# One scan step for both batches, with single large matmuls among its small tile products, in an RWKV-6 attention kernel

## The chip, the cores and the metric

The program runs on one core of one Trainium2 chip. The metric is the device time of one execution in microseconds (us). A core has five engines that run side by side and wait for each other through semaphores: PE (TensorE, matrix products into the PSUM banks), DVE (VectorE), ACT (ScalarE), POOL (GpSimd) and SP, which here only starts transfers.

## The reference

Two batches of 4096 tokens with 512 channels pass an attention layer and a feed-forward layer. Only the attention is touched. Cut to what matters:

```python
xw, xk, xv, xr, xg = [x + sx * mix[:, :, i] for i in range(5)]   # sx: the token before minus this one
r, k, v = xr @ Wr, xk @ Wk, xv @ Wv
g = jax.nn.silu(xg @ Wg)
w = jnp.exp(-jnp.exp(time_decay + jnp.tanh(xw @ td_w1) @ td_w2))
def step(state, rkvw):                     # 4096 tokens, 16 heads of 32 channels
    a = k_t[..., :, None] * v_t[..., None, :]
    y = jnp.einsum('bhk,bhkv->bhv', r_t, state + u[None, :, :, None] * a)
    new_state = w_t[..., :, None] * state + a
    return (new_state, y)
return normalised(y) * g @ Wo              # then x + ga * this, and the feed-forward layer
```

## The kernel before

The attention handles 32 chunks of 128 tokens, each for both batches. Iteration i of every engine's loop works on three chunks: it projects chunk i, runs the scan of chunk c = i - 1, and finishes chunk f = i - 2 (output product, residual). Each engine runs a fixed program; the order of its work is the order in which the body functions call the helpers, and semaphores hold it together.

The scan is done by groups of 32 tokens. Step n = 0 to 7 takes batch n // 4 and group n % 4. `pe_scores` multiplies keys by queries in 32x32 tiles of the array: 16 products of 80 columns (L406), 16 each of 48 and 16 (L410, L412), and 16 for the state's increment (L417), 64 in all. `dve_A` then assembles the 32x32 matrices `Am` from these scores with one product (L874) and seven predicated copies (L887), and updates the state (L881, L903). `pe_y` forms the output of the group in 32 tile products (L432, L435). The scores of odd and even n go to different PSUM banks (`SC[n % 2]`, `XB[n % 2]`), and `pe_scores(n)` waits for the assembly of n - 1 alone, so that scores for one step are formed while DVE assembles the one before.

Among the steps stand, on PE, whole 128x128 products: the g projection (`pe_g`, L512, two halves of eight matmuls), the output product (`pe_wo`, L525, four matmuls of 512 columns for each batch), the mixing products `pe_delta` (L466) and two decay products (L479, L486). After the steps come the transposes `pe_x` (L444), the k, r and v projections (L498), `pe_tm1` (L451, L454) and the scores of step 0 for the next iteration:

```python
            for n in range(1, 8):
                if do_w:
                    pe_scores(pe, c, n)
                    if n <= 2:
                        pe_g(pe, c, n - 1, do_p)
                    pe_y(pe, c, n - 1)
```

DVE's order around step 0 matters too: at the end of an iteration it transposes keys (L861), scales and transposes the normalised output (L920, L922), and only then begins the steps. The product with the gate, `dve_z` (L927), waits for ACT's affine step (L611).

Of the kernel before, what the change touches and what calls it, by code (L numbers as in the profile page):

```python
# [137 lines left out]
def attention(nc, x1, x, maa_x, maa, tm_w1, tm_w2, decay, td_w1, td_w2, faaaa, Wr, Wk, Wv, Wg, Wo,  # L138
              ln_w, ln_b, c_in, wmod, ident_in, diag_in, pick_in, ni=NI):
    with ExitStack() as ctx:  # L140
# [56 lines left out]
        s_tmp = sb("s_tmp", [P, G, K])  # L197
        Am = sb("Am", [P, 2, G, 32])
# [158 lines left out]
        score_done = sig("score_done", 8)  # L357
        A_step = sig("A_step", 8 * A_STEPS)
        A_done = sig("A_done", 8)
        s_step = sig("s_step", 8)  # L360
        state_done = sig("state_done", 8)
        y_done = sig("y_done", 8)
# [33 lines left out]
        def pe_scores(pe, c, n):  # L396
            b, q = divmod(n, Q)
            sc, scm = SC[n % 2], XB[n % 2]
            if n == 0:
                settled_after(pe, mod_done, (der, c), (ru_done, c), (m1_done, c), (k_done, c), (derk, c, 2))  # L400
            elif n >= 2:
                settled_after(pe, mod_done, (A_done, c, n - 1))
            for g in range(G):
                X = (g * B + b) * Q + q
                for d in HEADS:
                    nc.tensor.matmul(sc[d, g * NS:(g + 1) * NS], kvar[d, 0, g, b, 32 * q:32 * q + 32], rcol[d, X, 0:M1], start=True, stop=True)  # L406
            for g in range(G):
                X = (g * B + b) * Q + q
                for d in HEADS:
                    nc.tensor.matmul(scm[d, g * NM:g * NM + X0 - M1], kvar[d, 1, g, b, 32 * q:32 * q + 32], rcol[d, X, M1:X0], start=True, stop=True)  # L410
                for d in HEADS:
                    nc.tensor.matmul(scm[d, g * NM + X0 - M1:(g + 1) * NM], kvar[d, 2, g, b, 32 * q:32 * q + 32], rcol[d, X, X0:SEND], start=True, stop=True)  # L412
            if n == 0:
                settled_after(pe, mod_done, (vT_done, c), (kT_done, c))
            for g in range(G):
                for d in HEADS:
                    last = nc.tensor.matmul(sc[d, G * NS + g * K:G * NS + (g + 1) * K], kT[d, g, b, q, :], v_s[d, g, b, q, :], start=True, stop=True)  # L417
            last.then_inc(score_done.sem, 1)

        def pe_y(pe, c, n):  # L420
            b, q = divmod(n, Q)
            if n == 0:
                settled_after(pe, mod_done, (A_done, c, n + 1), (yT_done, c - 1))
            elif n == 4:
                settled_after(pe, mod_done, (A_done, c, n + 1), (yT_done, c, 1))
            else:
                settled_after(pe, mod_done, (A_done, c, n + 1))
            for g in range(G):
                X = (g * B + b) * Q + q
                for d in HEADS:  # L430
                    out = YB[d, g * P + 32 * q:g * P + 32 * q + 32]
                    nc.tensor.matmul(out, v_s[d, g, b, q, :], Am[d, n % 2, g, :], start=True, stop=False)  # L432
                for d in HEADS:
                    out = YB[d, g * P + 32 * q:g * P + 32 * q + 32]
                    last = nc.tensor.matmul(out, state[d, b, q, g, :], r32[d, X, :], start=False, stop=True)  # L435
            last.then_inc(y_done.sem, 1)
# [65 lines left out]
        def pe_g(pe, c, h, do_p):  # L502
            if h == 0:
# [12 lines left out]
        def pe_wo(pe, f, b, fenced, gated):  # L516
# [5 lines left out]
            if b == 1:  # L522
                after(pe, x1_done, f, 1)
# [1190 lines left out]
```

## Time and profile before

| | |
|---|---|
| median of 3 runs | 4346.82 us (4338.47 to 4366.6) |
| profiled execution | 4355.78 us, its span 4353.8 us |
| granted PE clock over the span | 0.931 of full speed |
| busy: PE, PE weight loads, DVE | 3775.7, 2595.8, 3517.6 us |
| busy: ACT, POOL | 1612.9, 1140.0 us |
| instruction queue | 538 packets, 8.81 MB |

The attention ends shortly after 2600 us; what follows is the preparation and the loop of the feed-forward layer. Every fp32 matmul shows as two records (two passes), each with its weight load, so 16 matmuls are "x32". Idle time with "issue" as its releaser is time in which the profile shows nothing that the engine waited for.

### The profile page before, as it was taken

To read this page: it belongs to the slowest core of one execution; us is meant where nothing else is said; L and a number is where in the kernel's file an instruction comes from. 1 tells how busy PE (TensorE), PEld (TensorE's weight loads), DVE (VectorE), ACT (ScalarE), POOL (GpSimd) and SP (SyncE) were. 2 spreads that over 40 slices of the span, in tenths; PEclk is the share of its full clock that TensorE was granted. 3 is DMA by queue.
4 is the path that set the end of the run, shared out by engine and by line. 5 is a ranking of instruction groups with operands and counts; after the bars stand their busy time and mean duration, and the time that the engine had idled before them with its cause. 6 is when DMAs were issued, how large, how long until landed. Compare 5 with 4: busy or idle time off the path is not lost. (4 is left out here: it accounts for less than half of the span.)

```text
span 4353.8 us, 155632 instructions
## 1 busy us (share of the span) xinstructions
PE 3775.7 (87%) x65992; PEld 2595.8 (60%) x65992; DVE 3517.6 (81%) x7798; ACT 1612.9 (37%) x3173; POOL 1140.0 (26%) x736
## 2 busy tenths in 40 slices
PE   4888898888898888888888873299999999999999
PEld 3767777676677776777767651145454545545454
DVE  4777788776788876788777757799999999999997
ACT  2434434344353442443434412233333333333333
POOL 1121121211212212122121113433333333333332
PEclk7989999999999998999999986599999999999999
DMA  3000000000000000000000003001011110111110
GB/s 112 13 22 27 18 32 18 23 27 18 23 27 23 27 18 23 27 21 29 18 23 27 13 22 114 15 23 37 31 37 32 36 38 30 37 30 37 38 30 30
DMA packets 73617, 133.45 MB, mean 31 GB/s; under 512 B 13248, under 2 KB 14016, under 8 KB 72896
## 3 DMA queue, kind: packets, MB, share of 16 engines
q1 hardware_dynamic: 72896, 123.13, 8.8%
q8 instruction: 538, 8.81, 0.9%
q14 instruction: 183, 1.50, 0.1%
HBM read 89.56 MB, written 33.55 MB: 28 GB/s over the span
## 5 line engine op out<-in xcount | busy, mean ns | idle before, releaser
L719 POOL TENSOR_TENSOR xf<-xf,hT 128x1024 f32<-128x1024 f32 x128 | 308.8, 2413 | 1190.6 <-DVE xf L769 1190.6
L887 DVE COPY_PREDICATED Am<-pick,banks 128x64 f32<-128x64 uint8 (+2 forms) x1792 | 459.6, 257 | 128.2 <-DVE Am L887 12.7
L1603 PE MATMUL fbank<-dT,hqT 128*128 128x512 f16 x2112 | 489.0, 380 | 20.8 <-ACT hqT L1520 20.6
L1591 PE MATMUL fbank<-gT,xqT 128*128 128x464 f16 (+1 forms) x2304 | 491.0, 363 | 11.5 <-issue 6.7
L1591 PE MATMUL fbank<-uT,xqT 128*128 128x464 f16 (+1 forms) x2304 | 488.2, 362 | 0.0
L730 POOL TENSOR_TENSOR yrs<-yvar,neg_half 128x32 f32<-128x32 f32 x32 | 174.0, 5438 | 839.7 <-DVE yvar L916 839.7
L1591 PEld LDWEIGHTS fbank<-gT,xqT 128*128 128x128 f16 x2304 | 225.6, 98 | 248.5 <-issue 12.6
L1531 ACT ACTIVATE sil<-fbank,und 128x464 f32<-128x464 f32 (+1 forms) x192 | 123.9, 646 | 656.6 <-PE fbank L1591 656.6
L1591 PEld LDWEIGHTS fbank<-uT,xqT 128*128 128x128 f16 x2304 | 225.7, 98 | 231.5 <-issue 1.1
L1603 PEld LDWEIGHTS fbank<-dT,hqT 128*128 128x128 f16 x2112 | 196.5, 98 | 236.2 <-ACT hqT L1520 31.4
L769 DVE SCALAR_TENSOR_TENSOR xf<-banks,col_maa,sx 128x256 f32<-128x256 f32 x640 | 265.3, 476 | 80.9 <-PE banks L466 80.8
L525 PE MATMUL banks<-w_o,yn 128*128 128x512 f32 x512 | 279.8, 696 | 18.0 <-DVE yn L927 15.9
L512 PE MATMUL banks<-xf,w_g 128*128 128x256 f32 x1024 | 266.9, 419 | 13.3 <-ACT gu L668 11.9
L1388 POOL TENSOR_TENSOR hq<-q16h,s16h 128x1408 f16<-128x1408 f16 x64 | 163.7, 2558 | 400.3 <-DVE hq L1380 400.3
L498 PE MATMUL banks<-xf,w_k 128*128 128x256 f32 x1024 | 251.0, 401 | 6.8 <-issue 5.0
L432 PE MATMUL banks<-Am,v_s 32*32 32x32 f32 x8192 | 191.9, 198 | 69.4 <-issue 67.8
L592 ACT ACTIVATE m_stack<-xxx 32x256 fp32r<-32x256 f32 x512 | 211.9, 414 | 99.5 <-DVE xxx L760 81.1
L435 PE MATMUL banks<-r,state 32*32 32x32 f32 x8192 | 191.9, 196 | 58.9 <-issue 58.8
L623 ACT ACTIVATE xxx<-xxx 128x1024 f32<-128x1024 f32 x32 | 33.8, 1057 | 563.0 <-DVE xxx L782 563.0
L512 PEld LDWEIGHTS banks<-xf,w_g 128*128 128x128 f32 x1024 | 208.9, 209 | 49.9 <-ACT gu L668 13.4
L874 DVE TENSOR_TENSOR Am<-banks,diag 128x128 f32<-128x128 f32 x256 | 72.3, 282 | 205.1 <-PE banks L417 200.8
L406 PE MATMUL banks<-rcol,kvar 32*32 32x80 f32 x8192 | 209.5, 238 | 25.1 <-issue 25.1
(237 smaller groups left out, 8483.3 us busy)
## 6 DMA issues: line engine op xcount, KB each, us to landing
x_tok<-in_L_attn_x SPq DMA_DIRECT2D x32, 512.0 KB, 3.8
xres<-in_L_attn_x SPq DMA_DIRECT2D x32, 512.0 KB, 3.5
x_after_attention<-xres SPq DMA_DIRECT2D x32, 512.0 KB, 3.7
xl<-x_after_attention SPq DMA_DIRECT2D x64, 256.0 KB, 2.7
xr<-x_after_attention SPq DMA_DIRECT2D x64, 256.0 KB, 2.7
out<-xr SPq DMA_DIRECT2D x64, 256.0 KB, 2.0
raw_g<-in_L_ffn_w_gate SPq DMA_DIRECT2D x1, 2816.0 KB, 10.9
raw_u<-in_L_ffn_w_up SPq DMA_DIRECT2D x1, 2816.0 KB, 14.0
```

What stands on the lines that cost most here:

```text
L406: nc.tensor.matmul(sc[d, g * NS:(g + 1) * NS], kvar[d, 0, g, b, 32 * q:32 * q + 32], rcol[d, X, 0:M1], start=True, stop=True)
L432: nc.tensor.matmul(out, v_s[d, g, b, q, :], Am[d, n % 2, g, :], start=True, stop=False)
L435: last = nc.tensor.matmul(out, state[d, b, q, g, :], r32[d, X, :], start=False, stop=True)
L498: last = nc.tensor.matmul(PROJ[h][:, (g % 2) * BT:(g % 2 + 1) * BT], w[:, k, g * P:(g + 1) * P], buf[:, k].rearrange("p b t -> p (b t)"), ...
L512: last = nc.tensor.matmul(SMALL[:, (g % 2) * BT:(g % 2 + 1) * BT], w_g[:, k, g * P:(g + 1) * P], xf[:, NMIX - 1, k].rearrange("p b t -> p ...
L525: last = nc.tensor.matmul(SMALL[:], yn[:, k, b, :], w_o[:, b, k, :], start=(k == 0), stop=(k == G - 1))
L592: last = nc.scalar.activation(m_stack[rows, j, :], m_part[part % 2][HEADS[f], 0, :], ACT.Copy)
L719: nc.gpsimd.tensor_tensor(xf[:, j % NXF].rearrange("p g b t -> p (g b) t"), xf[:, j % NXF].rearrange("p g b t -> p (g b) t"), hT[:, :, :, ...
L769: last = nc.vector.scalar_tensor_tensor(xf[:, j % NXF, g], PROJ[g // 2][:, (g % 2) * BT:(g % 2 + 1) * BT].rearrange("p (b t) -> p b t", b= ...
L887: nc.vector.copy_predicated(dst, mask, src).then_inc((done or A_step).sem, 1)
L1591: last = nc.tensor.matmul(GU[2 * pair + t][:, 0:w], xqT[:, u, a, g, :], W[:, b_, g, lo_:hi_], start=(k == 0), stop=(k == 3 * G - 1))
L1603: last = nc.tensor.matmul(DN[1 - u][:], hqT[:, a, kk, :], dT[:, b_, kk, :], start=(first and kk == 0), stop=(end and kk == KF - 1))
```

## The change

A scan step now takes one group of 32 tokens for both batches, so there are four steps q = 0 to 3 and not eight. `SC[0]`, `SC[1]` hold the scores of batch 0 and 1, `XB` is one bank for both, and `YB` becomes two banks, one per batch. `pe_scores(q)` waits for the assembly of q - 1. DVE's operations of a step are as many as before and twice as wide. `pe_g` and `pe_wo` give one matmul per call, and `pe_scores` and `pe_y` call them through `large(x)`, at eight places of a step. The copies of the output from PSUM (`act_yT`) both come after the last step, and the first half of the k projection moves behind the last step and the transposes.

```diff
-        PROJ, SC, YB = bank[2:4], bank[4:6], bank[7]
-        XB = (bank[0], bank[6])
-        XT = (bank[1], bank[6])
+        PROJ, SC, YB = bank[2:4], bank[4:6], bank[6:8]
+        XB = bank[0]
+        XT = (bank[1], bank[0])
...
+        def pe_scores(pe, c, q, large=None):
...
+            else:
+                settled_after(pe, mod_done, (A_done, c, q))
+            t = slice(32 * q, 32 * q + 32)
+            for b in range(B):
+                for g in range(G):
+                    X = (g * B + b) * Q + q
+                    for d in HEADS:
+                        nc.tensor.matmul(SC[b][d, g * P:g * P + NS], kvar[d, 0, g, b, t], rcol[d, X, 0:M1], start=True, stop=True)
...
+                    if large and g == 1:
+                        large(2 * b)
+                if large and b == 0:
+                    large(1)
...
+                if large and b == 0:
+                    large(3)
             last.then_inc(score_done.sem, 1)
...
+                    if g % 2:
+                        if b == 1 and g == G - 1:
+                            last.then_inc(y_done.sem, 1)
+                        if large:
+                            large(4 + 2 * b + g // 2)
...
+        def pe_g(pe, c, h, x, do_p):
+            if x == 0:
+                if h == 0:
+                    xf_wait(pe, c, NMIX - 1)
+                    after(pe, x1_done, c - 2)
+                    if do_p:
+                        after(pe, mf_done, c + 1)
+                else:
+                    after(pe, gu_done, c, 1)
+            g, k = 2 * h + x // 4, x % 4
+            last = nc.tensor.matmul(SMALL[:, (g % 2) * BT:(g % 2 + 1) * BT], w_g[:, k, g * P:(g + 1) * P],
...
+            def third(x):
+                if do_p and x == 1:
+                    pe_delta(pe, i, 3)
+                if do_f and x % 2:
+                    pe_wo(pe, f, 0, x // 2, do_p, do_w)
+
+            def fourth(x):
+                if do_f:
+                    pe_wo(pe, f, 1, x - 4, do_p, do_w)
+
             if do_p:
-                pe_proj(pe, i, 1, lambda h: after(pe, ww_done, i), (0,))
+                pe_delta(pe, i, 0)
             if do_w:
-                pe_y(pe, c, 7)
+                pe_scores(pe, c, 1, lambda x: pe_g(pe, c, 0, x, do_p))
+                pe_y(pe, c, 0, lambda x: pe_g(pe, c, 0, x, do_p))
+            if do_p:
+                pe_delta(pe, i, 1)
+            if do_w:
+                pe_scores(pe, c, 2, lambda x: pe_g(pe, c, 1, x, do_p))
+                pe_y(pe, c, 1, lambda x: pe_g(pe, c, 1, x, do_p))
+            if do_p:
+                pe_delta(pe, i, 2)
+                pe_td1(pe, i)
+            if do_w:
+                pe_scores(pe, c, 3, third)
+                pe_y(pe, c, 2, third)
...
+            if do_p:
+                pe_delta(pe, i, 4)
+            if do_w:
+                pe_y(pe, c, 3, fourth)
...
+            if do_p:
+                pe_td2(pe, i)
             if more:
                 pe_x(pe, i + 1)
             if do_p:
-                pe_proj(pe, i, 1, lambda h: after(pe, ww_done, i), (1,))
+                pe_proj(pe, i, 1, lambda h: after(pe, ww_done, i))
...
-            for n in range(8):
+            for q in range(Q):
                 if do_w:
-                    dve_A(dve, c, n)
-                if n == 1 and do_f:
+                    dve_A(dve, c, q)
+                if q == 0 and do_f:
                     dve_z(dve, f)
-                if 1 <= n <= 5 and do_p:
-                    dve_mix(dve, i, n - 1)
-                if n == 2 and more:
+                if do_p and q < 3:
+                    dve_mix(dve, i, q)
+                if q == 1 and more:
                     dve_ln(dve, i + 1)
-                if n == 4 and do_w:
+                if q == 2 and do_w:
                     dve_g(dve, c)
-                if n == 5 and do_f:
+                if q == 3 and do_f:
                     dve_out(dve, f, 0)
-                if n == 6 and do_p:
+                if do_p and q >= 2:
+                    dve_mix(dve, i, q + 1)
+                if q == 3 and do_f:
+                    dve_out(dve, f, 1)
+                if q == 3 and do_p:
                     dve_ww(dve, i)
```

PE's program from the scores of step 0 to the g projection, before (`banks<-v_s,kT` is L417's product, `[waits ...]` names semaphores):

```order
L417 MATMUL banks<-v_s,kT 32x32 [waits kT_done,vT_done,mod_done]
L417 MATMUL banks<-v_s,kT 32x32 x15
L406 MATMUL banks<-rcol,kvar 32x80 x16
...
L417 MATMUL banks<-v_s,kT 32x32 x16
L97 REGISTER_ALU
L512 MATMUL banks<-xf,w_g 128x256 [waits mf_done,x1_done,xf_done_p]
L512 MATMUL banks<-xf,w_g 128x256 x7
L116 ISA
L432 MATMUL banks<-Am,v_s 32x32 [waits yT_done,A_done,mod_done]
```

The same place of the changed program:

```order
L422 MATMUL banks<-v_s,kT 32x32 [waits kT_done,vT_done,mod_done]
L422 MATMUL banks<-v_s,kT 32x32 x31
L97 ISA [waits vT_done]
L473 MATMUL banks<-m_stack,w_tm 128x256 [waits m_stacked]
L473 MATMUL banks<-m_stack,w_tm 128x256 x3
L406 MATMUL banks<-rcol,kvar 32x80 [waits A_done,mod_done]
...
L410 MATMUL banks<-rcol,kvar 32x48 x4
L412 MATMUL banks<-rcol,kvar 32x16 x4
L97 REGISTER_ALU
L519 MATMUL banks<-xf,w_g 128x256 [waits mf_done,x1_done,xf_done_p]
L410 MATMUL banks<-rcol,kvar 32x48 x4
```

Before, step 1's scores and eight g matmuls stood between step 0's scores and the first wait for `A_done`. Now only one mixing product does, and the g matmuls stand one by one behind that wait. In a chunk PE goes from small tiles to a large product 25 times, before 9 times.

DVE's program of a step, before and then changed:

```order
L874 TENSOR_TENSOR Am<-banks,diag 128x128 [waits y_done,score_done]
L881 TENSOR_TENSOR s_tmp<-state,T 128x128 [waits state_done]
L108 ISA
L887 COPY_PREDICATED Am<-pick,banks 128x8x12 [waits A_step,mod_used]
```

```order
L900 TENSOR_TENSOR Am<-banks,diag 128x256 [waits y_done,score_done]
L906 TENSOR_TENSOR s_tmp<-state,T 128x256 [waits state_done]
L108 ISA
L912 COPY_PREDICATED Am<-pick,banks 128x16x12 [waits A_step,mod_used]
```

The operations of a step are the same, at twice the width, and there are four steps in a chunk.

## Rows read from the trace of the kernel before

**Rows 1.** The page's busy tenths and PE clock in 40 slices of the span.
```profile
PE   4888898888898888888888873299999999999999
PEclk7989999999999998999999986599999999999999
```

**Rows 2.** The line L910, once per chunk: duration min/median/max, first and last start.
```profile
L910 DVE STREAM_TRANSPOSE yS<-yT x32: 1235/1239/1246, 177.1 to 2602.2; 128x1024 f32<-128x1024 f32 x32
```

**Rows 3.** Busy time by stretch: length, PE, PEld, DVE, ACT, POOL, clock, DMA, GB/s.
```profile
177.10:2602.20 2425.10, 2112.08 (x55060) 1704.61 (x55057) 1852.63 (x4748) 965.24 (x2270) 485.09 (x209) 0.93 0.07 22
```

**Rows 4.** PE's waits in that stretch: releaser, total us, times, longest.
```profile
PE banks L432 <- issue: 62.9, 38, 2.4
...
PE banks L417 <- DVE kT L861: 23.1, 31, 0.7
...
PE banks L512 <- ACT gu L668: 11.9, 13, 1.7
...
PE banks L512 <- issue: 1.2, 3, 0.6
```

**Rows 5.** PE's timeline, start and length in us: a gap within one step's products.
```profile
1014.22 0.27 PE L432 MATMUL banks<-Am,v_s 32*32 32x32 f32 x3 [2.05 <-issue]
```

**Rows 6.** The page's instruction queue: packets, MB, share of the 16 engines.
```profile
q8 instruction: 538, 8.81, 0.9%
```

**Rows 7.** All transfers from 1085 to 1101 us, GB/s in slices of 0.4 us.
```profile
GB/s 0 0 41 0 0 0 0 0 0 0 0 0 41 0 0 0 0 0 0 0 0 41 0 113 328 328 389 123 26 5 0 0 41 0 0 0 0 0 0 0
```

**Rows 8.** PE's timeline across step 0's last products, step 1's scores, g and y.
```profile
1070.22 0.42 PE L417 MATMUL banks<-v_s,kT 32*32 32x32 f32 x29 [0.75 <-DVE kT L861]
...
1070.50 0.74 PE L406 MATMUL banks<-rcol,kvar 32*32 32x80 f32 x30
...
1071.67 0.44 PE L417 MATMUL banks<-v_s,kT 32*32 32x32 f32 x29
1072.07 3.70 PE L512 MATMUL banks<-xf,w_g 128*128 128x256 f32 x16
1075.69 0.26 PE L432 MATMUL banks<-Am,v_s 32*32 32x32 f32 x8
...
1076.38 0.74 PE L466 MATMUL banks<-m_stack,w_tm 128*128 128x256 f32 x4
```

**Rows 9.** DVE's timeline at the same place, up to step 0's last copies.
```profile
1068.87 1.20 DVE L861 STREAM_TRANSPOSE kT<-kvar 128x1024 f32<-128x1024 f32 x1
...
1071.21 1.25 DVE L922 STREAM_TRANSPOSE yn<-yS 128x1024 f32<-128x1024 f32 x1
1072.38 0.25 DVE L874 TENSOR_TENSOR Am<-banks,diag 128x128 f32<-128x128 f32 x1
...
1074.47 0.70 DVE L887 COPY_PREDICATED Am<-pick,banks 128x64 f32<-128x64 uint8 x2
```

**Rows 10.** DVE's groups by width: busy us and mean ns of one, idle before.
```profile
L887 DVE COPY_PREDICATED Am<-pick,banks 128x96 f32<-128x96 uint8 x496 | 137.6, 277 | 26.5 <-DVE Am L887 3.2 <-issue 0.7
L887 DVE COPY_PREDICATED Am<-pick,banks 128x32 f32<-128x32 uint8 x496 | 121.7, 245 | 48.9 <-DVE Am L887 3.2
L874 DVE TENSOR_TENSOR Am<-banks,diag 128x128 f32<-128x128 f32 x248 | 70.0, 282 | 201.2 <-PE banks L417 196.9 <-issue 3.9
```

**Rows 11.** The line L850, a product of 256 columns: duration min/median/max in ns.
```profile
L850 DVE TENSOR_TENSOR rcol<-rcol,T x32: 424/425/429, 120.8 to 2550.3; 128x256 f32<-128x256 f32 x32
```

**Rows 12.** A stretch at the lower clock, columns of Rows 3.
```profile
1041.30:1044.70 3.40, 3.40 (x21) 2.73 (x9) 3.33 (x7) 0.00 (x0) 0.00 (x0) 0.50 0.43 156
```

**Rows 13.** PE's timeline there and after: both halves of the k projection, the transposes.
```profile
1041.34 5.37 PE L498 MATMUL banks<-xf,w_k 128*128 128x256 f32 x16
...
1047.35 1.07 PE L444 MATMUL banks<-ident,xn 128*128 128x128 f32 x8
...
1048.25 3.62 PE L498 MATMUL banks<-xf,w_k 128*128 128x256 f32 x16
```

**Rows 14.** DVE's timeline at the end of the next chunk's steps: the decay operations.
```profile
1113.98 1.66 DVE L782 TENSOR_SCALAR xxx<-banks,col_decay 128x256 f32<-128x256 f32 x4
```

More of the change, by code:

```diff
@@ L393, in sp_body @@
                 sp.dma_start(x1[:, tok(f), :].rearrange("b t n -> t b n"), xres[:]).then_inc(x1_stored.sem, 16)
[L396 to L399, printed above, removed]
+        def pe_scores(pe, c, q, large=None):
+            if q == 0:
                 settled_after(pe, mod_done, (der, c), (ru_done, c), (m1_done, c), (k_done, c), (derk, c, 2))
[L401 to L413, printed above, removed]
[L414 to L418 removed]
@@ L500, in pe_proj @@
                 last.then_inc(proj_done.sem, 1)
-        def pe_g(pe, c, h, do_p):
-            if h == 0:
-                xf_wait(pe, c, NMIX - 1)
-                after(pe, x1_done, c - 2)
-                if do_p:
-                    after(pe, mf_done, c + 1)
-            else:
-                after(pe, gu_done, c, 1)
-            for g in (2 * h, 2 * h + 1):
-                for k in range(G):
-                    last = nc.tensor.matmul(SMALL[:, (g % 2) * BT:(g % 2 + 1) * BT], w_g[:, k, g * P:(g + 1) * P],
-                                            xf[:, NMIX - 1, k].rearrange("p b t -> p (b t)"), start=(k == 0), stop=(k == G - 1))
-            last.then_inc(proj_done.sem, 1)
@@ L516, in pe_wo @@
[L516 to L526 removed]
+        def pe_g(pe, c, h, x, do_p):
[9 more added lines that the diff above has]
+            last = nc.tensor.matmul(SMALL[:, (g % 2) * BT:(g % 2 + 1) * BT], w_g[:, k, g * P:(g + 1) * P],
+                                    xf[:, NMIX - 1, k].rearrange("p b t -> p (b t)"), start=(k == 0), stop=(k == G - 1))
+            if x == 7:
+                last.then_inc(proj_done.sem, 1)
@@ new lines, in pe_wo @@
+        def pe_wo(pe, f, b, k, fenced, gated):
+            if k == 0:
+                after(pe, z_done, f)
+                if b == 0 and fenced:
+                    after(pe, u1_done, f + 2)
+                elif b == 0 and gated:
+                    after(pe, gu_done, f + 1)
+                if b == 1:
+                    after(pe, x1_done, f, 1)
+            last = nc.tensor.matmul(SMALL[:], yn[:, k, b, :], w_o[:, b, k, :], start=(k == 0), stop=(k == G - 1))
+            if k == G - 1:
+                last.then_inc(wo_done.sem, 1)
@@ new lines, in pe_body @@
+            if do_p:
[4 more added lines that the diff above has]
+                pe_y(pe, c, 2, third)
+            else:
+                for x in range(8):
+                    third(x)
+            if do_p:
+                pe_delta(pe, i, 4)
+            if do_w:
+                pe_y(pe, c, 3, fourth)
+            else:
+                for x in range(4, 8):
+                    fourth(x)
+            if do_p:
+                pe_td2(pe, i)
```

125 lines of the change are left out of this document (51 added, 74 removed).

## The prediction

> **What bounds the kernel now.** I read the page first. PE is at eight to nine tenths through the whole attention, at a granted clock of mostly 0.9 [rows 1], so the question is what PE waits for and at which clock it runs. The line L910, which occurs once in a chunk, runs 32 times from 177.1 to 2602.2 us: 78.2 us for a chunk [rows 2]. In that stretch PE is busy for 2112 of 2425 us, DVE for 1853, ACT for 965, and the clock is 0.93 [rows 3]. PE's waits say who could be at fault. Only two lines name another engine with more than 5 us in total: 23.1 us for DVE's transposed keys and 11.9 us for ACT's copies of g. Beside these, twelve lines say "issue", from 62.9 down to 1.2 us, 271.7 us together [rows 4]. So PE is the bound: per chunk (divided by 31) it loses 0.75 us to DVE, 0.4 us to ACT and 8.8 us to "issue", and nearly nothing else.
>
> What "issue" is can be seen in the timeline. A gap of 2.05 us stands in the middle of a step's y products [rows 5], where no instruction waits. The instruction queue brought 8.81 MB in 538 packets, so a packet is a block of 16.4 KB [rows 6], or 256 instructions of 64 bytes. From 1085 to 1101 us the lone slices with 41 GB/s are such blocks: at slices 2, 12, 21 and 32, that is 3.6 to 4.4 us apart [rows 7]. I take it that a block does not come sooner than about 3.6 us after the one before, and that PE stalls when it uses up a block faster. It does: a step's scores are 64 matmuls, each with two passes and two weight loads, 256 instructions, and take 1.57 us (1070.50 to 1072.07); 16 records of g are 32 instructions and take 3.6 us; a y takes 0.69 us (1075.69 to 1076.38) [rows 8].
>
> Last the clock. From 1041.30 to 1044.70 us the granted clock is 0.50, the lower level of 1.2 GHz [rows 12], right after one of the idle gaps, and 16 records of the k projection take 5.37 us where 16 others take 3.62 [rows 13]. A mean clock of 0.93 means 14% of the time at the lower level, 10.9 us of a chunk. Less the tenth in which PE is idle anyway, half of it is lost: 4.8 us a chunk.
>
> **The change, part by part** (us per chunk; "now" is the changed kernel).
>
> *Work on PE.* The number of matmuls is the same. What is new is that large ones stand alone among tiles. At an entry the last tile products would have gone on until 1072.11, and g begins at 1072.07 [rows 8]. In a row of tiles the next starts about 0.18 before the end of the one before, so 0.14 is lost. At the exit, g takes 3.62 from its first start to the first y product, against 3.46 for 16 records of k (1048.25 to the next projection's start; its 3.62 less the overlap of 0.16) [rows 8, 13]: at most 0.16, of which I take half. So an entry costs 0.22, with bounds of 0 and 0.34. There are 25 entries for 9: 16 x 0.22 = **+3.5**.
>
> The Trainium skill has a rule that speaks against this change: "TensorEngine Tiling (Array Packing)", section Key Properties, says that a change of tiling mode, not only of the tile, drains the engine. By that rule, with nothing overlapped at an entry or an exit, the sum would be that of the third rival below. The row shows a partial overlap, so I stay with 0.22.
>
> *DVE's assembly.* A step before takes 2.8 us (1072.38 to 1075.17) [rows 9]. Its copies hold 448 columns; from 32 to 96 columns a copy grows by 32 ns, so 0.5 ns a column, and twice the width adds 0.22 us. A product of 128 columns takes 282 ns and one of 256 takes 425 [rows 10, 11]; three of these add 0.43. A step for both batches is thus 3.45 us, four are 13.8 where eight were 22.4. DVE saves 8.6 us of a chunk, and that is worth nothing by itself: it is not the bound.
>
> *The new wait.* Before, step 1's scores did not need step 0's assembly, since they had banks of their own. Now they do. In the times of the trace: the first tile products of step 0 ended at 1069.47 (0.75 before 1070.22) [rows 8]; with both batches they end 1.25 later, at 1070.7. The key products take 0.6, the one mixing product 0.7: PE is through at 1072.0. DVE begins the assembly at 1072.38, as before, since its transposes stand in front of it, and ends at 1075.8 [rows 9]. PE waits 3.8 us, where it had step 1's scores and eight g matmuls to do. **+3.8**. Queued behind this wait are all g matmuls and with them ACT's copies, which have time until the two decay products of step 2. It also takes the place of the wait for the keys, **-0.75**, and g's second half no longer waits for ACT, **-0.4**.
>
> In the later steps PE has 3.9 us of y and g and 0.7 of mixing to do while DVE assembles for 3.45, so these waits are covered. Three small ones are not: for ACT's g before the decay products, for DVE's mixing inside step 3, for the first residual before the last output product. I set **+0.5** for them, bounds 0 and 2. At the end of the steps PE needs the decay operations before it may begin the k projection: 1.66 us of DVE [rows 14] against 0.9 us of transposes (1047.35 to 1048.25) [rows 13]. Before, a step's products covered that: **+0.85**.
>
> *Instruction blocks.* The same 14 or so blocks a chunk. A batch's scores with two large matmuls take 1.5 + 2 x 0.66 = 2.8 us for one block, 0.8 less than the 3.6 that the next needs. Of the six such blocks of steps 1 to 3 the first is there already, after PE's long wait. 5 x 0.8 = 4.0. A y block for both batches, with four large ones and a mixing product, takes 4.6 and causes no stall. With 0.9 for blocks that fall badly: 4.9 where 8.8 were, **-3.9**. Bounds: 1.5 (the spacing is really nearer 3 us) and 7.
>
> *Clock.* The gaps within the steps become shorter than 1 us; the one of 0.75 at 1070.22 was followed by g at full speed [rows 8]. The new wait of 3.8 is longer than any of those gaps, and I expect one stretch of 3.4 us at the lower level after it, in every chunk: half of it lost, 1.7 where 4.8 were, **-3.1**. Bounds: 0.5 and 4.8.
>
> Sum: 3.5 + 3.8 - 0.75 - 0.4 + 0.5 + 0.85 - 3.9 - 3.1 = +0.5 us a chunk, times 31 = +16 us. The profiled execution took 4355.8 us, which becomes 4372; it was 9 us above the median of 4346.8, so the forecast for the median is **4363 us**. The feed-forward part, some 1700 us, is not touched.
>
> **The rivals.**
>
> *1. The large matmuls cover the blocks, and the clock stays up: faster.* If a block needs only 3 us, the stalls fall to 1.5, and if the stretch at the lower level falls into scores that wait for blocks anyway, the clock costs 0.5. That is 3.4 and 1.2 less than in my sum: -4.1 a chunk, -127 us, 4220; halfway there it is 4290. For it: in rows 7 the blocks are 3.6 apart where PE had stalled, so a part of that may be PE's own. Against: the stall before step 1's scores remains.
>
> *2. The wait for step 0's assembly keeps the clock down: slower.* The place is step 1. If the stretch at the lower level after that wait lasts through its g matmuls and returns after the next stalls, the clock costs as much as before: +3.1 more, +3.6 a chunk, +112 us, 4459. It decides from two such stretches a chunk on. For it: idle gaps of 2 us were enough before [rows 5, 12]. Against: g matmuls are spread over the two steps that follow, and gaps become short.
>
> *3. Every entry is a full stop.* Tiles end before a large matmul starts and it ends before the next tile: 0.18 + 0.22 + 0.38 = 0.78 where 0.44 is its share in a row, 0.34 an entry, 5.5 for 16. That is +2.0 more, +2.5 a chunk, +78 us, 4425. Against: g began 0.04 before the tiles' end [rows 8]. This is the case that the rule of the Trainium skill above would give.
>
> *4. The order of work gives another wait that I did not see,* on ACT or DVE at the end of the steps, where both copies of the output now stand ahead of the decay's exponentials. It would show as slower, by 1 to 3 us a chunk; I count it with rival 2.
>
> **How the numbers follow.** The forecast gets 0.37, rival 1 0.32, rivals 2 and 4 0.20, rival 3 0.11. A measurement here tells about 1% from no change, that is 4303 to 4390 us, the forecast's own range. Faster by more than that: rival 1, 0.32. Within it: 0.37. Slower: 0.31. The range takes in most of rival 1 and all of 2 and 3: 4235 to 4470.
>
> **What would show it.** In the changed profile: PE waits for DVE's copies before L406 once a chunk, 3.8 us, over 110 us in all (if under 60, that step fails). Waits put down to "issue" fall from 272 to about 150 us. The clock in the attention rises from 0.93 to 0.97; if it stays at 0.93, rival 2. A step's scores with their four large matmuls take 5.5 us from first to last at full clock; 6.0 or more and rival 3 holds. The k projection begins 0.85 us after the transposes. The distance of the transposes of y is 78.7 us a chunk. The prediction is wrong if the blocks come in another rhythm when large matmuls stand among the tiles, since that is read from stalled stretches alone.

## The result, and the profile after

The changed kernel takes 4434.85 us (median of 4 runs, 4427.2 to 4440.67) against 4347.2 for the kernel before: a ratio of 1.018, 95% interval 1.015 to 1.021. It is slower by 1.8%, inside the stated range (4235 to 4470) and 72 us above the forecast of 4363; it lies beyond the 4303 to 4390 that the prediction gave to the forecast itself.

The runs below were made in three sets. The kernel before, run again beside each, took 4341.88, 4359.71 and 4359.6 us, so differences of some 20 us between runs of different sets are not told apart; the ratios, each to the kernel before of its own set, are the better measure. One of the four executions of the kernel with pairs below took 6857 us at a mean clock of 0.79 where the others showed 0.94, and its ratio leaves that execution out.

The line that stands once in a chunk, transposing y, in the changed kernel (answers to [rows 2]):

```profile
L935 DVE STREAM_TRANSPOSE yS<-yT x32: 1232/1233/1236, 177.0 to 2672.5; 128x1024 f32<-128x1024 f32 x32
```

A chunk takes 80.5 us and took 78.2. The two stretches differ by 70.4 us, and the spans of the profiled executions by 71.3: the whole loss is in the attention. (The medians differ by 88, since the profiled execution of the kernel before was 9 us above its median and that of the changed kernel 8 below.) The stretch between these two times, with the columns of [rows 3]:

```profile
177.00:2672.50 2495.50, 2197.53 (x55074) 1653.49 (x55072) 1652.93 (x3523) 960.99 (x2275) 507.65 (x209) 0.94 0.07 22
```

DVE is busy 200 us less, 6.4 us a chunk, and it bought nothing. PE is busy 85 us more. PE's waits in the changed kernel (total us, times, longest; answers to [rows 4]):

```profile
PE banks L406 <- DVE Am L912: 110.8, 31, 4.7
PE banks L422 <- issue: 51.5, 53, 2.1
PE banks L505 <- DVE xxx L809: 25.9, 30, 1.9
PE banks L486 <- ACT gu L696: 23.5, 30, 0.8
PE banks L438 <- issue: 18.9, 26, 1.4
PE banks L412 <- issue: 17.0, 15, 1.6
PE banks L410 <- issue: 14.3, 15, 1.7
PE banks L436 <- issue: 12.9, 23, 1.4
PE banks L473 <- ACT m_stack L620: 5.3, 3, 1.9
PE banks L473 <- issue: 5.2, 2, 3.7
PE banks L473 <- ACT m_stack L623: 4.0, 1, 4.0
...
```

The first line is the new wait: once in each chunk the scores of step 1 wait for the last predicated copies of step 0. All lines of "issue" sum to 124 us, where they were 272. The waits for the keys and for ACT ahead of g's second half are gone; waits for ACT's g (L696) and for its stack (L620, L623) have come.

The timeline of PE and of DVE around that wait (answers to [rows 8] and [rows 9]):

```profile
1178.55 0.74 PE L422 MATMUL banks<-v_s,kT 32*32 32x32 f32 x64
...
1179.22 0.74 PE L473 MATMUL banks<-m_stack,w_tm 128*128 128x256 f32 x4
...
1183.68 1.29 PE L406 MATMUL banks<-rcol,kvar 32*32 32x80 f32 x32 [3.72 <-DVE Am L912]
...
1185.40 1.22 PE L519 MATMUL banks<-xf,w_g 128*128 128x256 f32 x2
```
```profile
1178.41 1.25 DVE L947 STREAM_TRANSPOSE yn<-yS 128x1024 f32<-128x1024 f32 x1
1179.58 0.39 DVE L900 TENSOR_TENSOR Am<-banks,diag 128x256 f32<-128x256 f32 x1
...
1182.57 0.96 DVE L912 COPY_PREDICATED Am<-pick,banks 128x128 f32<-128x128 uint8 x2
```

DVE begins step 0's assembly at 1179.58, 0.3 after PE's last key product (1178.55 + 0.74), and needs until 1183.53; PE is idle from the mixing product to 1183.68. After it 32 records of L406 take 1.29 us and a g matmul 1.22, where they take 0.76 and 0.70 further down. The clock there and in the stretch after (columns of [rows 3], answers to [rows 12]):

```profile
1182.56:1189.38 6.82, 5.70 (x140) 4.36 (x144) 4.19 (x9) 3.35 (x10) 0.00 (x0) 0.52 0.01 2
1189.40:1196.70 7.30, 7.29 (x290) 5.22 (x284) 4.06 (x12) 0.57 (x2) 0.00 (x0) 1.00 0.02 4
```

The lower level begins in the last 1.3 us of this wait and lasts for 5.5 us of the work after it. Each of the 31 waits has such a stretch at its end or right behind it, 3.4 to 10.2 us long and 8.1 on average; in several chunks a shorter stall stood just before the wait as well. Only about 1 us a chunk of the lower level lies elsewhere.

Last, singles among tiles at full clock, in y of step 0:

```profile
1193.36 0.70 PE L519 MATMUL banks<-xf,w_g 128*128 128x256 f32 x2
1193.99 0.26 PE L436 MATMUL banks<-Am,v_s 32*32 32x32 f32 x8
1194.08 0.24 PE L438 MATMUL banks<-r,state 32*32 32x32 f32 x8
1194.14 0.24 PE L436 MATMUL banks<-Am,v_s 32*32 32x32 f32 x8
1194.20 0.24 PE L438 MATMUL banks<-r,state 32*32 32x32 f32 x8
1194.38 0.70 PE L519 MATMUL banks<-xf,w_g 128*128 128x256 f32 x2
```

From one single's start to the next tiles it takes 0.63 us, where a matmul in a row of them takes 3.62 / 8 = 0.45 [rows 8]: 0.18 lost at the exit. Parts of a step's scores with four singles, in step 2 of a later chunk, which ran at full clock and without a gap that the profile shows:

```profile
1359.78 0.76 PE L406 MATMUL banks<-rcol,kvar 32*32 32x80 f32 x32
...
1363.08 0.23 PE L412 MATMUL banks<-rcol,kvar 32*32 32x16 f32 x8
1363.14 0.27 PE L410 MATMUL banks<-rcol,kvar 32*32 32x48 f32 x8
1363.23 0.23 PE L412 MATMUL banks<-rcol,kvar 32*32 32x16 f32 x8
1363.38 0.70 PE L519 MATMUL banks<-xf,w_g 128*128 128x256 f32 x2
1364.01 0.29 PE L410 MATMUL banks<-rcol,kvar 32*32 32x48 f32 x8
...
1364.33 0.47 PE L422 MATMUL banks<-v_s,kT 32*32 32x32 f32 x32
1364.73 0.70 PE L519 MATMUL banks<-xf,w_g 128*128 128x256 f32 x2
1365.36 0.67 PE L422 MATMUL banks<-v_s,kT 32*32 32x32 f32 x32
```

After a group of L412 the next tiles of a row start 0.06 later (1363.08 to 1363.14); the g matmul starts 0.15 later (1363.23 to 1363.38): 0.09 lost at the entry. So one single costs about 0.27 us. The last line shows something else: 32 records of L422 take 0.67 there and 0.47 one line above, 0.2 us lost inside a row of tiles where the profile shows no gap.

**The ledger used below.** A chunk is split as follows, from the trace: its length; PE's waits put down to "issue"; the wait for step 0's assembly; all idle time of PE; the time lost to the clock (the time at the lower level in which PE is not idle, halved: before, 11.2 us at that level less 0.8 idle, gives 5.2); and the rest, which is PE's work at full clock with whatever gaps are too short to show between overlapping tile products. "Entries" is how often in a chunk PE goes from tiles to a large product, counted in the traces; for the kernel before it is 10, and not the 9 that stands with the change, so the change adds 15. The ratio is that to the kernel before of the same set.

| kernel | median us | ratio | entries | chunk | issue | step 0's assembly | all idle | clock | rest |
|---|---|---|---|---|---|---|---|---|---|
| before | 4347 | 1 | 10 | 78.2 | 8.8 | 0 | 10.1 | 5.2 | 63.0 |
| changed | 4435 | 1.018 | 25 | 80.5 | 4.0 | 3.6 | 9.6 | 3.6 | 67.3 |
| changed, DVE's transposes later | 4409 | 1.015 | 25 | 80.1 | 3.9 | 3.0 | 9.0 | 3.8 | 67.3 |
| changed, large ones in one piece | 4516 | 1.039 | 8 | 83.6 | 8.1 | 3.6 | 13.7 | 7.9 | 62.0 |
| changed, eight g matmuls first | 4396 | 1.012 | 18 | 79.7 | 7.7 | 0.35 | 9.3 | 5.7 | 64.7 |
| changed, pairs | 4435 | 1.017 | 15 | 80.7 | 7.0 | 3.6 | 12.6 | 3.5 | 64.6 |
| changed, pairs, four first | 4418 | 1.014 | 14 | 80.15 | 9.2 | 1.55 | 12.9 | 2.6 | 64.7 |
| changed, fewer instructions | 4266 | 0.980 | 25 | 75.3 | 1.4 | 4.25 | 7.4 | 2.3 | 65.6 |
| before, singles | 4382 | 1.008 | 28 | 79.0 | 5.0 | 0 | 7.4 | 3.7 | 67.9 |
| before, pairs | 4286 | 0.983 | 18 | 76.3 | 5.1 | 0 | 8.5 | 2.3 | 65.5 |
| before, fewer instructions | 4188 | 0.962 | 10 | 72.6 | 3.8 | 0 | 8.3 | 2.5 | 61.8 |
| before, with the wait | 4492 | 1.030 | 10 | 82.65 | 7.3 | 4.7 | 13.1 | 6.9 | 62.7 |
| before, pairs spread over step 3 | 4229 | 0.970 | 18 | 74.05 | 4.3 | 0 | 6.7 | 1.8 | 65.6 |

The trace also tells what "issue" is. In the kernel before, 133 gaps of over 0.8 us lie ahead of a tile product in this stretch; 132 of them end 2.1 to 2.9 us after the start of a block's transfer in the instruction queue. In the changed kernel it is 69 of 71, the wait for step 0's assembly not counted. Moments so placed make up only 14% of the time. And the blocks keep a distance: of 439 spacings before, two are below 3.2 us and the median is 4.2; in the changed kernel the shortest is 3.3 and the median 4.1.

Theory: the single placing by itself about pays for its entries in fewer stalls for instruction blocks and a steadier clock; the loss is the wait for step 0's assembly, which one set of score banks brings. Rival: the entries are the loss.

### The profile page after: what moved, and what is told of

Same layout as the page of the kernel before. It is cut to its first block and busy times, and to the rows that moved or that the text cites. A ratio compares the mean times of both kernels' runs of the same rounds, so it can differ in the third digit from the quotient of the medians.

```text
span 4425.1 us, 152216 instructions
## 1 busy us (share of the span) xinstructions
PE 3864.2 (87%) x65992; PEld 2543.6 (57%) x65992; DVE 3307.8 (75%) x6518; ACT 1605.0 (36%) x3173; POOL 1162.3 (26%) x736
## 5 line engine op out<-in xcount | busy, mean ns | idle before, releaser
L519 PE MATMUL banks<-xf,w_g 128*128 128x256 f32 x1024 | 397.5, 472 | 2.6 <-issue 2.4
L757 POOL TENSOR_TENSOR yrs<-yvar,neg_half 128x32 f32<-128x32 f32 x32 | 198.8, 6214 | 661.0 <-DVE yvar L941 661.0
L1618 PEld LDWEIGHTS fbank<-gT,xqT 128*128 128x128 f16 x2304 | 225.6, 98 | 248.9 <-issue 13.1
L912 DVE COPY_PREDICATED Am<-pick,banks 128x128 f32<-128x128 uint8 (+2 forms) x896 | 318.7, 356 | 62.3 <-DVE Am L912 4.1
L406 PE MATMUL banks<-rcol,kvar 32*32 32x80 f32 x8192 | 227.2, 253 | 115.4 <-DVE Am L912 113.9
L695 ACT ACTIVATE gate<-banks 128x512 f32<-128x512 f32 x64 | 38.2, 598 | 707.2 <-PE banks L519 707.2
L900 DVE TENSOR_TENSOR Am<-banks,diag 128x256 f32<-128x256 f32 x128 | 53.7, 419 | 313.3 <-PE banks L422 309.4
L406 PEld LDWEIGHTS banks<-rcol,kvar 32*32 32x32 f32 x8192 | 173.0, 117 | 197.9 <-issue 192.6
L436 PEld LDWEIGHTS banks<-Am,v_s 32*32 32x32 f32 x8192 | 155.4, 107 | 185.4 <-issue 181.7
L505 PE MATMUL banks<-xf,w_k 128*128 128x256 f32 x1024 | 229.7, 382 | 25.9 <-DVE xxx L809 25.9
L620 ACT ACTIVATE m_stack<-xxx 32x256 fp32r<-32x256 f32 x512 | 211.9, 414 | 101.7 <-DVE xxx L787 83.1
L410 PE MATMUL banks<-rcol,kvar 32*32 32x48 f32 x8192 | 230.9, 216 | 15.2 <-issue 15.2
```

The source lines that it names most:

```text
L406: nc.tensor.matmul(SC[b][d, g * P:g * P + NS], kvar[d, 0, g, b, t], rcol[d, X, 0:M1], start=True, stop=True)
L410: nc.tensor.matmul(XB[d, o:o + X0 - M1], kvar[d, 1, g, b, t], rcol[d, X, M1:X0], start=True, stop=True)
L505: last = nc.tensor.matmul(PROJ[h][:, (g % 2) * BT:(g % 2 + 1) * BT], w[:, k, g * P:(g + 1) * P], buf[:, k].rearrange("p b t -> p (b t)"), ...
L519: last = nc.tensor.matmul(SMALL[:, (g % 2) * BT:(g % 2 + 1) * BT], w_g[:, k, g * P:(g + 1) * P], xf[:, NMIX - 1, k].rearrange("p b t -> p ...
L620: last = nc.scalar.activation(m_stack[rows, j, :], m_part[part % 2][HEADS[f], 0, :], ACT.Copy)
L757: nc.gpsimd.tensor_tensor(yrs[:], yvar[:], neg_half[:], ALU.pow).then_inc(yrs_done.sem, 1)
```

## The experiments

**The wait itself, moved.**

```diff
# end of the DVE body
-            if do_w:
-                dve_yn(dve, c)
# after step 0's assembly in the next iteration
                 if q == 0 and do_f:
+                    dve_yn(dve, f)
                     dve_z(dve, f)
```

> The changed kernel, but DVE scales and transposes the normalised output (2.4 us) after step 0's assembly, not ahead of it. Theory (the loss is PE's wait for step 0's assembly, 3.6 us a chunk, and the lower clock after it): the assembly starts 2.4 us earlier, the wait falls to about 1.2 us a chunk, the clock in the attention rises to 0.96 or more, and the time falls by 75 us for the wait and 0 to 50 for the clock: 4310 to 4360 us. Rival (the loss is the price of single large matmuls among tiles): the wait falls as well, but PE then only stalls for instruction blocks instead, and the time stays within 25 us of 4435.

Measured: 4409.41 us, ratio to before 1.015 (1.012 to 1.018). The theory's time did not come: the median fell by 25 us, the ratio by 0.003 and the attention of the profiled execution by 12.5, which is within the scatter between sets, and the wait fell only from 3.6 to 3.0 us a chunk. The rival had the time right to within a microsecond, but no stalls for blocks came in the wait's place (3.9 us of "issue" as before). The traces of this kernel show why:

```profile
1171.81 0.74 PE L422 MATMUL banks<-v_s,kT 32*32 32x32 f32 x64
...
1176.71 1.29 PE L406 MATMUL banks<-rcol,kvar 32*32 32x80 f32 x32 [3.50 <-DVE Am L912]
```
```profile
1172.60 0.43 DVE L900 TENSOR_TENSOR Am<-banks,diag 128x256 f32<-128x256 f32 x1 [1.73 <-PE banks L422]
```

DVE is idle for 1.73 us and starts when PE's key products end (1172.55). With the transposes out of the way the assembly begins 0.05 us after the last key product in every chunk; it is then held by the scores of both batches, and PE by the assembly. In the changed kernel itself it begins 0.7 us after them on average: in 18 of the 31 chunks DVE's transposes still hold it up, mostly by 1.1 to 1.2 us. So the transposes are worth 0.6 us of the wait and not the 2.4 that I took for it. What is left is the assembly's 3.8 to 3.9 us less one mixing product.

**The large matmuls in one piece, in the changed kernel.**

```diff
-                pe_scores(pe, c, 1, lambda x: pe_g(pe, c, 0, x, do_p))
-                pe_y(pe, c, 0, lambda x: pe_g(pe, c, 0, x, do_p))
+                pe_scores(pe, c, 1)
+                for x in range(8):
+                    pe_g(pe, c, 0, x, do_p)
+                pe_y(pe, c, 0)
```

(the same for step 2 and the output product)

> The changed kernel with both batches per step, but the large matmuls in one piece: eight g matmuls between a step's scores and its y, the output product behind the scores of step 3 and behind the last y. Theory (an entry into a large matmul among tiles costs 0.25 to 0.3 us and gives about as much back in fewer stalls for instruction blocks): 4 us a chunk less PE work, stalls put down to issue up from 4.0 to 7 or 8 us a chunk, time 4410 to 4470 us. If single placing is the loss: stalls stay near 4 and the time falls by 100 us or more. If single placing is what pays: the stalls reach 9 to 10 us and the time is 4500 us or more.

Measured: 4515.91 us, ratio 1.039 (1.036 to 1.042). The rest falls by 5.3 us, as the entries fall from 25 to 8: 0.31 us for each, not 0.22. The stalls double and the clock costs 4.3 more. That is the outcome foreseen for "single placing pays" in the time, with stalls between the two cases. So within the new form of the scan, placing singly is worth 81 us by the medians and 95 by the length of the attention; against one piece it isn't the loss.

**Singles alone, in the kernel before.**

```diff
+                wo = {5: lambda x: x % 2 and pe_wo(pe, f, 0, x // 2, do_p, do_w), 7: lambda x: x % 2 and pe_wo(pe, f, 1, x // 2, do_p, do_w)}
+                large = (lambda x: pe_g(pe, c, n - 1, x, do_p)) if n <= 2 else wo.get(n) if do_f else None
                 if do_w:
-                    pe_scores(pe, c, n)
-                    if n <= 2:
-                        pe_g(pe, c, n - 1, do_p)
-                    pe_y(pe, c, n - 1)
+                    pe_scores(pe, c, n, large)
+                    pe_y(pe, c, n - 1, large)
```

(with one call of `large` after each column group of tiles; DVE's first residual one step later)

> The kernel before (eight steps, one batch each, two sets of score banks), with the large matmuls placed singly: the g matmuls among the tiles of steps 1 and 2, the output product's among those of steps 5 and 7. Theory (singles take about as much in entries as they give back in block stalls; the loss of the change is the wait for step 0's assembly): stalls put down to issue fall from 8.8 to 5 or 6 us a chunk, PE's work rises by 4 to 5 us, time 4310 to 4390 us. Rival (the entries are the loss): stalls fall by less than 2 us a chunk and the time rises to 4430 us or more.

Measured: 4381.5 us, ratio 1.008 (1.006 to 1.011). The time is as the theory had it. The rest rises by 4.9 for 18 entries more, 0.27 for each, the stalls fall by 3.7, the clock costs 1.4 less: a small loss. Of the change's 88 us, some 40 are thus there without the new scan form, though not with the same places and with 28 entries for 25.

**The wait alone, in the kernel before.**

```diff
-            elif n >= 2:
-                settled_after(pe, mod_done, (A_done, c, n - 1))
+            else:
+                settled_after(pe, mod_done, (A_done, c, max(n - 1, 1)))
```

> The kernel before, with one wait added: step 1's scores wait for step 0's assembly, as in the changed kernel, though their banks are free. Theory (this wait is what the change loses by): PE waits 4.5 us a chunk there (from 1070.5 to 1075.2 in the old trace), of which about 1 comes back in stalls for blocks, since the queue fills meanwhile: 3 to 4.5 us a chunk, 4440 to 4490 us. Rival (the wait only moves stalls that would come anyway): the stalls put down to issue fall by 3 us or more and the time rises by less than 40 us.

Measured: 4491.97 us, ratio 1.030 (1.028 to 1.033), at the upper end of the expected span. PE's first line of waits in this kernel:

```profile
PE banks L406 <- DVE Am L887: 146.5, 31, 6.9
PE banks L432 <- issue: 63.1, 35, 2.5
```

4.7 us a chunk of wait, 1.4 less in stalls, and the clock costs 6.9 where it cost 5.2; the granted clock of the attention is 0.90 in this kernel. A wait of 4.7 us makes the chunk 4.4 us longer. This is the price of having no second set of score banks at step 1, and it is of the size of the change's loss and more. What the change gives beside it (fewer stalls in the steps, no wait for the keys) brings part of it back. The changed kernel with a second set of score banks for step 1 was not run, so in the changed kernel itself the wait's price is inferred.

**Filling the wait.** Eight g matmuls in one piece in front of step 1's scores:

```diff
+                for x in range(8):
+                    pe_g(pe, c, 0, x, do_p)
-                pe_scores(pe, c, 1, lambda x: pe_g(pe, c, 0, x, do_p))
-                pe_y(pe, c, 0, lambda x: pe_g(pe, c, 0, x, do_p))
+                pe_scores(pe, c, 1)
+                pe_y(pe, c, 0, lambda x: pe_g(pe, c, 1, x - 4, do_p))
```

> The changed kernel, but the first eight g matmuls stand in one piece ahead of step 1's scores, where PE waits for step 0's assembly; the second eight stand singly in step 1's y and step 2's scores. Theory: the 3.6 us wait is filled with 3.5 us of g at full clock, the lower clock after it goes, and 1 to 1.5 us of new wait comes for ACT's copy of g ahead of the second half: 2 to 4 us a chunk, 4310 to 4370 us. Rival (single placing is the loss): half of it goes here too, eight entries fewer at 0.3 us, 75 us, so this run tells less than the other three; it would then gain about 75 us and not more.

Measured: 4396.24 us, ratio 1.012 (1.009 to 1.016), so neither the expected 4310 to 4370 us nor the rival's 75 us: 39 less by the medians. The wait falls to 0.35, and the stalls go from 4.0 back to 7.7: what is taken out of the steps is missed there. The clock costs 5.7, so the lower level does not come from the long wait alone: in this trace its stretches of 3.4 to 13.7 us mostly follow stalls of 1.5 to 2.5 us among bare tiles.

**Pairs, in the changed kernel:** two g matmuls at every second place.

```diff
+            def two(h, x):
+                if x % 2:
+                    pe_g(pe, c, h, x - 1, do_p)
+                    pe_g(pe, c, h, x, do_p)
```

> The changed kernel with the large matmuls two by two: a pair of g matmuls at every second place, the last output product as two pairs. Ten entries fewer in a chunk. Theory (an entry costs 0.3 us, by the 5.2 us of work between single placing and one piece over 16 entries; what covers an instruction block is the large matmuls' time and not their number): work down by 3 us a chunk, stalls put down to issue up by 1 at most, time 4350 to 4390 us. Rival (a stretch of tiles between two large matmuls must be short): stalls rise by 3 us or more, time stays at 4435.

Measured: 4434.9 us, ratio 1.017 (1.014 to 1.020). The rest falls by 2.7 for 10 entries fewer, the stalls rise by 3.0: the rival's outcome. With four of them in front of step 1's scores besides:

```diff
+                for x in range(4):
+                    pe_g(pe, c, 0, x, do_p)
+                pe_scores(pe, c, 1, lambda x: x == 2 and two(0, 5))
+                pe_y(pe, c, 0, lambda x: x == 5 and two(0, 7))
```

> As the pairs, and besides four of the first eight g matmuls in one piece in front of step 1's scores, where PE waits 3.6 us for step 0's assembly; the other four as pairs in step 1's scores and y. Theory: the wait falls to 1.8 us a chunk, the stalls for blocks rise by less than 1 us, since the queue is full after the wait: 1 to 2.5 us a chunk less than the pairs, 4290 to 4350 us. Rival (as in the run with eight g matmuls in front: every large matmul taken out of the steps comes back as a stall): within 20 us of the pairs.

Measured: 4418.01 us, ratio 1.014 (1.012 to 1.017). The wait falls by 2.0, the stalls rise by 2.2, and the time is within 20 us of the pairs: the rival's outcome again. In all three runs PE's work or wait shrinks and the chunk hardly does. Either the steps are held by something that runs beside PE, or my reading of "issue" is wrong.

**Fewer instructions, the same columns.** One product of 64 columns instead of those of 48 and 16, with the first's weights, so the 16 columns hold other values; in the kernel before, and then in the changed one.

```diff
-                    nc.tensor.matmul(scm[d, g * NM:g * NM + X0 - M1], kvar[d, 1, g, b, 32 * q:32 * q + 32], rcol[d, X, M1:X0], start=True, stop=True)
-                for d in HEADS:
-                    nc.tensor.matmul(scm[d, g * NM + X0 - M1:(g + 1) * NM], kvar[d, 2, g, b, 32 * q:32 * q + 32], rcol[d, X, X0:SEND], start=True, stop=True)
+                    nc.tensor.matmul(scm[d, g * NM:(g + 1) * NM], kvar[d, 1, g, b, 32 * q:32 * q + 32], rcol[d, X, M1:SEND], start=True, stop=True)
```

> The kernel before with one product of 64 columns in place of the two of 48 and 16 in the scores (it uses the first one's weights for both, so the 16 columns hold other values): the same columns, 16 matmuls of 64 fewer in a step, 512 of some 3600 instructions of a chunk. Theory (stalls put down to issue are waits for blocks of 256 instructions): two of 14 blocks go, stalls fall from 8.8 to between 5 and 7 us a chunk, time 4230 to 4290 us. Rival (the stalls come from something else in PE, such as register and semaphore instructions ahead of a step): stalls stay at 8 to 9 us and the time falls by less than 25 us.

Measured: 4188.38 us, ratio 0.962 (0.959 to 0.964). Two blocks fewer a chunk (the instruction queue brings 12.2 where it brought 14.2) make it 5.7 us shorter: 5.0 of it stalls, 2.7 clock, 1.2 less work, while 3.2 us of other waits come up. The time fell below the expected span, since I had left out the clock.

> The changed kernel with one product of 64 columns in place of the two of 48 and 16 in the scores, as in the run of that kind on the kernel before (the 16 columns hold other values). Theory (the changed kernel's steps are held by instruction blocks too, which hides part of its stalls inside the tile products): the time falls by 2 to 4 us a chunk, though only 4.0 us a chunk are put down to issue: 4310 to 4375 us. Rival (single large matmuls cover the blocks already): less than 1 us a chunk, 4400 us or more.

Measured: 4266.01 us, ratio to the kernel before 0.980 (0.977 to 0.983), so 169 us below the changed kernel, more than expected: 5.2 us a chunk, though only 4.0 had been put down to "issue". The stalls fall by 2.6, the clock costs 1.3 less, and the rest, too, falls by 1.7. The steps of both kernels are held by the arrival of instructions, and in the changed one a part of that shows as longer rows of tiles rather than as gaps, as in the row of 0.67 us above. The wait for step 0's assembly rises to 4.25.

**Towards a version that beats both:** two sets of score banks as before, and pairs.

```diff
+        WO_AT = {(4, 3): (0, 0), (4, 7): (0, 1), (5, 3): (0, 2), (5, 7): (0, 3), (6, 7): (1, 0), (7, 1): (1, 1), (7, 4): (1, 2), (7, 7): (1, 3)}
+                def large(x):
+                    if n <= 2 and do_w and x % 2:
+                        pe_g(pe, c, n - 1, x - 1, do_p)
+                        pe_g(pe, c, n - 1, x, do_p)
+                    if do_f and (n, x) in WO_AT:
+                        pe_wo(pe, f, *WO_AT[n, x], do_p, do_w)
```

> The kernel before (eight steps, double score banks) with g matmuls in pairs among the tiles of steps 1 and 2, and the output product's eight spread singly over steps 4 to 7. Theory: against the singles in the kernel before 8 entries less at 0.3 us, 2.4 us a chunk, block stalls as there (5.0) or 1 us more: 4300 to 4350 us, equal to the kernel before or faster by up to 1%. Rival (placing costs what it saves, however it is done): 4370 us or more.

Measured: 4286.04 us, ratio 0.983 (0.981 to 0.986), faster than both, and below the expected span. Against the singles: 10 entries fewer and 2.3 us less of the rest, 0.23 for each; stalls the same, I take it because the output product now covers four steps and not two; the clock costs 1.4 less. Pairing and spreading were changed together, and no run takes them apart.

```diff
+        G_AT = [(1, 1), (1, 3), (1, 5), (1, 7), (2, 5), (2, 7), (3, 1), (3, 3)]
-                    if n <= 2 and do_w and x % 2:
+                    if do_w and (n, x) in G_AT:
```

> The kernel before with pairs, but the g matmuls spread on: the first eight over step 1, the second eight from step 1's y over step 3's scores, so that they don't wait for ACT's copy of the first (1.4 us a chunk with the pairs). Theory: that wait goes, block stalls in steps 2 and 3 stay or fall by up to 1 us: 1 to 2 us a chunk less than the pairs, 4225 to 4265 us. Rival (the blocks take over): within 15 us of the pairs, 4286 us.

Measured: 4228.68 us, ratio 0.970 (0.966 to 0.973), as expected, and the fastest version with every product in place: 131 us less than the kernel before of its set, some 206 less than the changed kernel. Its once-a-chunk line and stretch:

```profile
L924 DVE STREAM_TRANSPOSE yS<-yT x32: 1235/1237/1248, 177.1 to 2472.6; 128x1024 f32<-128x1024 f32 x32
```
```profile
177.10:2472.60 2295.50, 2087.42 (x55060) 1637.57 (x55058) 1885.63 (x4749) 963.83 (x2271) 484.08 (x209) 0.97 0.07 24
```

The clock is 0.97, and the wait for ACT's g fell from 1.4 to 0.3 us a chunk before g's second half.

## Why the prediction was right in its range and short in its sum

The range was wide enough to take in rivals 2 and 3, and the outcome lies there, where the prediction had put a chance of 0.31. The sum is short by 1.8 us a chunk, 55 us; the other 17 of the 72 us come from which executions were profiled (9 above the median before, 8 below it after).

| term, us a chunk | forecast | measured |
|---|---|---|
| wait for step 0's assembly | +3.8 | +3.6 |
| waits for the keys, for ACT before g | -1.15 | -1.1 |
| decay operations before the k projection | +0.85 | +0.84 |
| small waits (ACT's g, ACT's stack) | +0.5 | +1.0 |
| stalls for blocks | -3.9 | -4.8 |
| clock | -3.1 | -1.5 |
| entries (measured: all that the rest rises by) | +3.5 | +4.3 |
| sum | +0.5 | +2.3 |

*What bounds it.* PE with its instruction blocks, as read: DVE's 6.4 us less changed nothing (8.6 were forecast; a step's assembly takes 3.9 us and not 3.45, since twice the width costs a copy 89 to 126 ns, 245 to 334, 250 to 339 and 277 to 403, which the slope between 32 and 96 columns did not tell). The reading of "issue" as waits for blocks was tested by the two runs with fewer instructions and by the times at which blocks arrive, and holds. So does the rhythm: blocks came no closer with large matmuls among the tiles than before. What the forecast had as a list of separate stalls is in fact one limit: take work from PE within the steps and stalls come in its place.

*The new wait.* Its size was right: 110.8 us in all, with over 110 named as the sign. So was its place. I held the assembly's start to be set by DVE's transposes, 1.1 us after the key products (1072.38 against 1071.3 in the times of the prediction). They set it in 18 of the 31 chunks, mostly by just that much; in the others the scores of both batches set it. The 75 us or more that the run with the transposes moved was to gain overlooked how close the scores stand behind them.

*The step that failed is the clock term, mis-sized.* "One stretch of 3.4 us at the lower level after it, in every chunk": the trace has 9.1 us a chunk at that level, of which 1.8 are idle, and 8.1 of the 9.1 stand at or behind this wait. So the clock gave back 1.5 and not 3.1, and its mean in the attention rose to 0.94 and not to 0.97. That is the mechanism of the second rival at half its price, and the kernel before with that wait alone shows it: the clock there costs 1.8 more than without it.

*The entries* are the second term that was sized too low, in spite of a count that was one too high (15 are added and not 16, so 0.22 would have given 3.3). The runs differ by 0.23 to 0.31 us for an entry, and the rows above give 0.27 for a single one, between the 0.22 that I took and the 0.34 of a full stop in the third rival. In the trace the two passes of a lone matmul start 0.32 us apart (median of 593), in a row 0.22. The rule of the Trainium skill ("TensorEngine Tiling (Array Packing)", Key Properties: a change of tiling mode drains the engine) speaks for a full stop; the trace agrees in so far as every entry and every exit costs time, but less than a full stop would. The sign given for this was badly set: 5.5 us for a step's scores with four large matmuls is less than the prediction's own terms make (2 x 1.57 + 4 x 0.66 = 5.8). The four such steps of the changed kernel that ran at full clock and without a gap of 0.2 us take 6.3 to 6.4 us, so by the sign rival 3 would hold; in the one shown above, 0.2 of its 6.26 is a slow row of tiles.

The loss is settled as to its main part: the wait is shown by adding it alone to the kernel before, the entries and the block stalls by taking the placing alone and undoing it alone. Two comparisons of like placing say the same: with pairs the new scan form has a chunk of 80.7 us and the old one 76.3, with singles 80.5 and 79.0. Not settled is how the 4.3 us of "rest" split between entries (15 at 0.27 would be 4.1) and short waits for blocks inside rows of tiles; the run with fewer instructions took 1.7 off the changed kernel's rest and 1.2 off that of the kernel before.

## What to carry to other kernels

Where an engine is fed by a limited stream of instructions, cover short instructions with long ones evenly, and try pairs where each switch has a price (with two sets of score banks they went with a gain, in the changed kernel they brought nothing); but do not give up a second set of buffers for it. Look at every wait that a merged step adds, and ask what the engine did in that time before. And when several remedies each remove a few us and the loop does not get shorter, look for one limit that runs beside all of them.

## What the runs showed of the hardware

- Instructions reach the core in blocks of 16.4 KB. In the changed kernel's attention no two blocks started less than 3.3 us apart, in the kernel before two of 439 spacings were below 3.2; of PE's gaps of over 0.8 us among tiles, 132 of 133 before and 69 of 71 after ended 2.1 to 2.9 us after the start of a block. 512 instructions fewer a chunk, with the same columns, made the chunk 5.7 us shorter in one kernel and 5.2 in the other.
- A single fp32 matmul of 256 columns among 32x32 tile products takes 0.63 us from its start to the next tiles, against 0.45 in a row; with 0.09 at its start that is 0.27 us, and per entry the kernels differ by 0.23 to 0.31 us.
- In the last 1.3 us of a wait of 3.7 us, and for 5.5 us after it, the clock was at the lower level; on average the attention's clock was 0.90 with a 4.7 us wait in each chunk, 0.93 without it, and 0.97 in the kernel with pairs spread over step 3, where PE is idle least.
- A predicated copy took 245, 250 and 277 ns with 32, 64 and 96 columns, and the same copies for both batches 334, 339 and 403 ns with 64, 128 and 192: at 64 columns both 250 and 334 were measured, so the number of columns alone does not set the time.
